# Four conditioned layers on one core: the feature-sum products behind the next gate products, the closing logarithm and root behind the seventh activation

## What is computed

```python
def _swiglu(x, gate_w, hidden_w, out_w, out_b):
    return jax.nn.silu(x @ gate_w.T) * (x @ hidden_w.T) @ out_w.T + out_b
...
x = x + a_alpha * _attention(...)
return x + f_alpha * _swiglu(_ada_rmsnorm(x, t, ffn_gamma_w, ffn_beta_w), gate_w, hidden_w, out_w, out_b)
...
mean = jnp.mean(input, axis=-1, keepdims=True)
var = jnp.mean(jnp.square(input - mean), axis=-1, keepdims=True)
out = (input - mean) * jax.lax.rsqrt(var + EPS) * weight + bias
out = out + tar_bias
return out * weight + bias
```

## Time and profile before

| what | value |
|---|---|
| median of 3 runs | 1068.98 us (1066.23 to 1071.0) |
| span of the profiled execution | 1062.0 us |
| PE busy | 1024.9 us, 97%, 5397 matmuls |
| DVE busy | 753.0 us, 71% |
| ACT busy | 637.4 us, 60% |
| GpSimd (POOL) busy | 176.2 us, 17% |
| feature-sum products L1822 and L1823 | 14 each, from 813.7 to 1038.0 us |
| table loads in the feed-forward steps | 17 of 1.28 us (9 at L1027, 6 at L1052, 2 at L1030) |

### The profile page before, as it was taken

The page is one execution under the profiler, slowest core; times in us unless marked ns, Lnnn a source line. Parts: engine busy times, 40 slices in busy tenths (PEclk is TensorE's granted clock), DMA queues, the critical chain, the costliest instruction groups (busy, mean ns, idle before and its releaser), DMA issues.

```text
span 1062.0 us, 16530 instructions
## 1 busy us (share of the span) xinstructions
PE 1024.9 (97%) x5397; PEld 636.6 (60%) x5397; DVE 753.0 (71%) x1211; ACT 637.4 (60%) x867; POOL 176.2 (17%) x203
## 2 busy tenths in 40 slices
PE   7999999999999999999999999999999999999996
PEld 6776667777543444434444444434487777878784
DVE  5867668888877877787877878789765466555654
ACT  5556323353376777786777777677753564555545
POOL 0000001221231233232333334021310000000000
PEclk9999999999999999999999999999999999999998
DMA  9978633215434353734445363634210000000001
GB/s 287 381 184 237 174 95 110 41 35 173 105 123 103 103 150 75 207 79 157 99 132 127 95 179 77 185 80 116 79 28 1 20 1 21 20 20 20 1 20 40
DMA packets 92041, 110.95 MB, mean 104 GB/s; under 512 B 47184, under 2 KB 57424, under 8 KB 90960
## 3 DMA queue, kind: packets, MB, share of 16 engines
q1 hardware_dynamic: 60736, 100.56, 32.4%
q10 hardware_dynamic: 31248, 9.65, 5.2%
HBM read 65.81 MB, written 33.03 MB: 93 GB/s over the span
## 4 chain that ended last, share of the span: by engine, by line
PE 68%; DVE 11%; ACT 5%; issue 4%; DMA 2%; ACTq 1%; SPq 1%; POOL 0%; DVEq 0%; POOLq 0%
PE st_ps L1766 13%; PE st_ps L1622 9%; PE mx_ps L1766 7%; PE av_ps L1604 7%; PE val_ps L1479 5%; PE gate_ps L1479 5%; DVE mx L1196 5%; PE misc_ps L1535 4%; PE misc_ps L1642 3%; PE mx_ps L1559 3%; PE misc_ps L1655 2%; PE y_ps L1489 2%; DVE stage L1205 2%; PE misc_ps L1646 1%; DVE xres L1389 1%
## 5 line engine op out<-in xcount | busy, mean ns | idle before, releaser
L1196 DVE TENSOR_REDUCE mx<-mx_ps 128x1 f32<-128x512 f32 x488 | 314.4, 684 | 101.1 <-PE mx_ps L1559 99.5
L1559 PE MATMUL mx_ps<-kring,qring 48*128 48x512 f32 x500 | 199.7, 461 | 4.2 <-DVE mx L1196 2.2
L1622 PE MATMUL st_ps<-qring,kring 50*128 50x512 f32 x512 | 186.7, 444 | 3.5 <-ACT shared L919 3.4
L1622 PEld LDWEIGHTS st_ps<-qring,kring 50*128 50x128 f32 x512 | 76.2, 184 | 146.2 <-issue 112.1
L919 ACT ACTIVATE pbuf<-st_ps 128x1024 f32<-128x1024 f32 x128 | 129.3, 1023 | 41.7 <-PE st_ps L1622 40.1
L919 ACT ACTIVATE shared<-st_ps 128x1024 f32<-128x1024 f32 x128 | 127.9, 1021 | 38.2 <-PE st_ps L1622 37.3
L1559 PEld LDWEIGHTS mx_ps<-kring,qring 48*128 48x128 f32 x500 | 84.7, 183 | 31.0 <-DVE mx L1196 26.0
L1373 DVE TENSOR_TENSOR shared<-st_ps,shared 128x512 f32<-128x512 f32 x64 | 44.1, 689 | 80.4 <-PE st_ps L1766 61.8
L1043 ACT ACTIVATE p_hi<-shared 128x512 fp32r<-128x512 f32 x64 | 40.4, 631 | 71.8 <-DVE shared L1373 71.2
L1259 DVE SCALAR_TENSOR_TENSOR h<-val_ps,r,gelu 128x1024 f32<-128x1024 f32 x32 | 41.0, 1282 | 47.9 <-PE val_ps L1479 47.9
L1382 DVE TENSOR_TENSOR p_lo<-shared,p_hi 128x512 fp32r<-128x512 f32 x64 | 45.1, 705 | 37.7 <-ACT p_hi L1043 37.0
(11 more groups left out here) (239 smaller groups left out, 2062.9 us busy)
## 6 DMA issues: line engine op xcount, KB each, us to landing
chunk<-in_gen_w SPq DMA_DIRECT2D x8, 2048.0 KB, 9.2
qring<-q_parts SPq DMA_DIRECT2D x64, 192.0 KB, 3.5
kring<-k_parts SPq DMA_DIRECT2D x64, 192.0 KB, 4.6
q_parts<-stage SPq DMA_DIRECT2D x16, 512.0 KB, 2.9
k_parts<-stage SPq DMA_DIRECT2D x16, 512.0 KB, 2.8
xres<-in_xT SPq DMA_DIRECT2D x8, 512.0 KB, 11.5
shared<-in_x SPq DMA_DIRECT2D x8, 512.0 KB, 12.3
q_parts<-stage SPq DMA_DIRECT2D x16, 256.0 KB, 3.0
```

Of the source, the lines that this page charges most:

```text
L1196: nc.vector.tensor_reduce(mx[h // GH % 2][:, col:col + 1], mx_ps[:, qt % 2], AX, ALU.max).then_inc(S["mx_free"], 1)
L1559: nc.tensor.matmul(out, qring[h // GH][r:r + QROWS, h % GH // 2, qt * P:(qt + 1) * P], kring[h // GH][r:r + QROWS, h % GH // 2, :], start= ...
L1622: ins = nc.tensor.matmul(st_ps[half][:, kt % 2], kring[g][r:r + SROWS, i % GH // 2, kt * P:(kt + 1) * P], qring[g][r:r + SROWS, i % GH // ...
```

## The change

On PE the two feature-sum products move from behind the output products of f = 2 and f = 5 to behind the gate products of f = 3 and f = 6. On ACT the table load, Ln and Exp move from behind p_hi(5) and the identity to behind silu(6), ahead of p_hi(6). DVE, GpSimd and the queues have the same instructions in the same order.

```diff
@@ ACT, the step of the feed-forward
                         nc.scalar.activation(silu[f % 2], fgate_ps[f % 2], ACT.Silu).then_inc(F["silu"], 1)
+                    if f == 6 and ends:
+                        if not (isinstance(b, int) and b == 1):
+                            nc.scalar.preload_act_table_set("natural_log_exp_and_others")
+                        wait_ffn(act, "stat", 2 * b)
+                        nc.scalar.activation(rstd, av_ps[:], ACT.Ln, bias=eps5[:]).then_inc(F["ln"], 1)
+                        wait_ffn(act, "ln", b)
+                        nc.scalar.activation(rstd, rstd, ACT.Exp, scale=-0.5).then_inc(F["rstd"], 1)
...
-                    if f == 5 and ends:
-                        if not (isinstance(b, int) and b == 1):
-                            nc.scalar.preload_act_table_set("natural_log_exp_and_others")
-                        wait_ffn(act, "stat", 2 * b)
-                        nc.scalar.activation(rstd, av_ps[:], ACT.Ln, bias=eps5[:]).then_inc(F["ln"], 1)
-                        wait_ffn(act, "ln", b)
-                        nc.scalar.activation(rstd, rstd, ACT.Exp, scale=-0.5).then_inc(F["rstd"], 1)
@@ PE, the step of the feed-forward
                         gate(b, f, rows)
+                    if f in (3, 6) and ends:
+                        if isinstance(b, int) and b == 1:
+                            wait(pe, "oaug", NG * NB)
+                        wait_ffn(pe, "sum_lo", 2 * b - 1 + f // 6)
+                        nc.tensor.matmul(av_ps[:], mean_r[:], sum_lo[:], start=True, stop=False)
+                        nc.tensor.matmul(av_ps[:], mean_r[:], sum_hi[:], start=False, stop=True) \
+                            .then_inc(F["stat"], 1)
...
-                    if f in (2, 5) and ends:
-                        if isinstance(b, int) and b == 1:
-                            wait(pe, "oaug", NG * NB)
-                        wait_ffn(pe, "sum_lo", 2 * b - 1 + f // 5)
-                        nc.tensor.matmul(av_ps[:], mean_r[:], sum_lo[:], start=True, stop=False)
-                        nc.tensor.matmul(av_ps[:], mean_r[:], sum_hi[:], start=False, stop=True) \
-                            .then_inc(F["stat"], 1)
```

## The result

| | before | changed |
|---|---|---|
| median, first comparison | 1069.99 us (4 runs, 1066.23 to 1073.44) | 1056.72 us (4 runs, 1053.56 to 1061.52) |
| ratio, first comparison | | 0.9884, interval 0.9848 to 0.992 |
| median, second comparison | 1067.07 us (12 runs, 1062.62 to 1074.8) | 1058.88 us (7 runs, 1053.63 to 1063.99) |
| ratio, second comparison | | 0.9906, interval 0.9872 to 0.9941 |
| span of the profiled execution | 1062.0 us | 1056.7 us |

What follows compares the result with a forecast made beforehand. TensorE's product spacing plus its standing bounds the kernel. Savings 3.1 + 1.9 + 0.5 + 0.98 + 1.36 + 1.63 = 9.4 us, ScalarE's part nothing; 1068.98 - 9.4 = 1059.6 us, range 1056.5 to 1063.5 us.

Steps and rivals of the forecast that it cites:

- What bounds the stage: Feed-forward: TensorE, busy 97% of the span, sets the time by its products 0.2267 us apart plus the places where it stands.
- The regular places: The 12 feature-sum places of items 2 to 7: waits and slower products behind them, 3.1 + 1.9 + 0.5 us, all go.
- the second rival: Feature-sum products cost something wherever they stand: 2.1 us stay, up to 5 with late-sequencer gaps; gain 4.5 to 7; 13%.
- Item 1, f = 2 and f = 5: Feature-sum pairs of item 1: 0.98 us of standing goes at f = 2; at f = 5, 1.36 of 2.22 us.
- The clock: Behind item 1, f = 5: TensorE's clock no longer falls after the shorter standing, saving 1.63 us on 12 products.
- the first rival: Item 1: the clock falls all the same, so the gain is 7.8 us and the time 1061.2 us; 20%.
- ScalarE, no cost: Logarithm and root behind silu(6) cost TensorE nothing, even with three more table loads in item 1, where slack is 3.3 us.
- slack 5.1 us and more: Regular items: reserve of the longer ScalarE chain before TensorE needs p_lo(6) at out(6) and silu(7) at gate(9).
- seven times nothing: ScalarE's later logarithm and root, and DVE's multiplication by rstd behind them, make no next TensorE product late.
- The distance between span and run: Median of runs 1068.98 us, 7.0 above the 1062.0 us span; left as it is when forming the forecast time.
- The slower rival: ScalarE's chain behind gate(6), 5.8 us, bounds every item; slower from 12.6 us, at 14 us 1078.5 us; 2%.
- The fourth rival: Earlier start given back at each item's end, where out(0) waits for the update of x; gain 0 to 2 us; 4%.

## Why the prediction was right, and where not

It said 1059.6 us, 9.4 us less, and the kernel measured 1056.7 and 1058.9 us in the two comparisons, 13.3 and 8.2 us less; the stretch that the change touches became 9.5 us shorter. The mechanism was right, and some of the closeness is luck. The 9.5 us are 9.0 us of standing and clock, 0.4 less than the sum, and 0.5 us of scatter behind them. And the first median lies only 0.2 us above the lower end of the range, 1056.5 us. Point by point:

- **What bounds the stage:** right. PE keeps its spacing of 0.227 us, and 8.99 us are gone ahead of the last output, standing and the slow stretch behind one of them. The other 0.5 us lie behind it (13.02 to 12.49 us). That tail measured 12.49 and 11.97 us in two profiles of the changed kernel itself, and 12.0 to 13.0 us over all profiles, so 0.5 us there is within the scatter.
- **The regular places:** 3.1 + 1.9 + 0.5 = 5.5 us were forecast, 5.4 without the rounding of the terms. The first pair of item 2 and that of item 7 are 172.15 us apart before (852.51 to 1024.66) and 168.00 now (853.76 to 1021.76): 0.83 us an item, 5.0 us for six. The mis-sized term is the 0.5 us for the slower products behind a pair, which I took to go whole. Only 0.2 us of it went and 0.3 us stayed: the 12 products behind a pair take 2.74 us with no wait ahead of them, not 2.72 (and behind two of the twelve places they had taken 2.74 before too). The remaining 0.1 us of the miss is 0.006 us of the pair's own at each place, and rounding. So the second rival holds with some 0.03 us a place, where it said 0.15; its 0.11 us inside the pair were due to the wait, and its gaps kept by a late sequencer were wrong.
- **Item 1, f = 2 and f = 5:** 0.98 and 1.36 us right, by the two kernels with one pair moved and by the 0.86 us that stay. The kernel behind the hidden products took those too.
- **The clock:** 1.63 us is its price when it falls (280.31 - 278.67 = 1.64), and it didn't fall behind the shorter standing in any of eight profiles, so the first rival was wrong. But the term holds for some executions only: with the long standing it fell in three of five. In a mean over executions it is worth about 1 us by this count, an estimate, and I booked it in full, since the one profile of before was one in which it fell. The change's gain is then some 8.3 us in the mean.
- **ScalarE, no cost:** right for the change, with the three loads, whose chain came to 8.3 us. But "slack 5.1 us and more" and "seven times nothing" were worked out for an item with another one behind it. In item 7, out(7) comes with 0.44 us in hand, which I hadn't looked at; that it cost nothing was luck. The row of a load, 1.28 us and 0.02 us to the next activation, decided the size of a switch. The Trainium skill (ScalarE: Activation LUTs, What ACT_TABLE_LOAD costs) adds a drain of some 1.38 us to each load, and the trace doesn't agree: none stands at the four loads shown. Item 1 with one load less is as fast.
- **ScalarE, no gain:** not quite. "Seven times nothing" was worked out with both edits made; I never worked out TensorE's edit without ScalarE's: there the move is worth 0.8 us, once, at the end of the last item.
- **The distance between span and run:** the step "7.0 us above the span; I leave that distance as it is" was wrong in what it says. The changed kernel's profiled execution took 1058.62 us with a span of 1056.7, 1.9 us more, and in all runs on record the distance is 1.8 to 2.1 us. Of before's 7.0 us some 5 were thus a profiled execution that was quicker than the median, by its clock in the attention part. The sum didn't suffer, since the difference was formed on the stage; the range's share for scatter was meant for such a case.
- **The slower rival:** its mechanism is real, its price was too low. "A chain of 12.6 us or more decides it" went by the reserve at gate(9). Four more Ln make the chain 8.7 us, and the kernel was still 4.5 us faster than before to the last output. Ten more Ln make the chain 5.8 + 7.2 = 13.0 us, by the rival 7 x (13.0 - 11.3) - 9.4 = 2.5 us slower than before; the kernel took 1094.64 us in its one run, 27.6 us above the 1067.07 us of before (26.6 us to the last output). TensorE stood ahead of output products, never of gate(9). The lateness runs on to out(0) of the next item, where the reserve is 0.4 us (update of x done at 850.64, out(0) at 851.04 us in the change), and is paid at both places. The fourth rival had named this place, as a point at which gain could be lost; it lost none, since update and output move together as long as ScalarE isn't late.

## What to carry to other kernels

Where an engine with no idle time waits 0.1 to 0.4 us for an operand again and again, put independent work of the same engine that is due anyway between the operand's last use and the wait; the gain is the sum of the stands, and it can be read from distances between starts. When a chain on a side engine is moved or made longer, follow it past the next due point to the following ones: a reserve of 5 us at one consumer doesn't help at another that stands behind the same queue with 0.4 us. Follow it into the last turn of the loop too, where no next item's work lies between. And compare stages from a common starting point when executions differ more ahead of the change than the change is worth.

## What was not expected of the hardware

After the same standing of TensorE, 2.35 us between two starts, with the same program, the clock fell to its lower level (16 products in 5 us) in one execution and stayed (24 products) in the next. In the kernel with ten more Ln TensorE stops nine times for 2.0 to 2.1 us within one execution, and the clock fell behind one of them. The same happens on a larger scale in the attention part, where the mean clock from 300 to 350 us was 1.00 (before), 0.88 and 0.81 (the change, twice), and over all profiles the start of the next stage came 762.7 to 775.0 us after the first instruction. One or two profiles of a kernel thus can't tell what a fall of the clock costs or whether an edit removes it.
